# Four graph layers on one core: middle biases moved from TensorE to VectorE, a leak made of two exponentials, unsplit scores, spread weight splits and new orders

## The reference

```python
# layer 0: hypergraph convolution, H = (adj != 0)
h = relu(Dn * (H @ (Be * (H.T @ (x @ W1.T)))) + b1);  h = layer_norm(h) * gamma + beta
y = Dn * (H @ (Be * (H.T @ (h @ W2.T)))) + b2 + x
# layer 1: GCN with tanh;     tanh(dinv * A @ dinv * (x @ W) + b)
# layer 2: attention
s = (x @ w) @ a;  A = s[:, None] + s[None, :];  A = tanh(A / 8) * 8
A = where(A >= 0, A, 0.1 * A);  A = exp(A) * adj;  A = A / A.sum(-1) * adj.sum(-1);  out = A @ x @ w
# layer 3: three adjacency products with a weight each, biases after each, relu after the first two
x1 = relu(adj @ (x @ W1) + b1);  x2 = relu(adj @ (x1 @ W2) + b2);  out = adj @ (x2 @ W3) + b3
```

## Time and profile before

| | |
|---|---|
| median of 3 runs | 1438.51 us |
| the profiled execution | 1435.79 us |
| its span, first to last instruction | 1433.8 us |
| mean granted TensorE clock | 0.995 |
| busy: PE, DVE, ACT, POOL | 1392.3, 1287.9, 990.5, 947.7 us |
| instructions: PE, DVE, ACT, POOL | 10900, 4001, 2312, 1876 |

### The profile page before, as it was taken

One profiled execution on the slowest core, in us unless ns is written; L12 is line 12 of the kernel. 1 busy time (PEld: TensorE's weight loads), 2 busy tenths in 40 slices (PEclk: granted clock), 3 DMA queues, 4 the chain that ended last, 5 costly groups with the idle time before them and its releaser, 6 DMA issues.

```text
span 1433.8 us, 34585 instructions
## 1 busy us (share of the span) xinstructions
PE 1392.3 (97%) x10900; PEld 1331.7 (93%) x10900; DVE 1287.9 (90%) x4001; ACT 990.5 (69%) x2312; POOL 947.7 (66%) x1876
## 2 busy tenths in 40 slices
PE   3799999999999999999999999999999999999997
PEld 2799999999999999999999999999999999999996
DVE  5789999999999999999999999999999999999984
ACT  3577777777777777777777777777777777777763
POOL 2676676676676676676676676676676676676652
PEclk9999999999999999999999999999999999999999
DMA  7011110120110110110110110110110110110100
GB/s 187 1 42 27 52 51 26 51 51 26 51 51 26 51 51 26 51 51 26 51 51 26 51 51 26 51 51 26 51 51 26 51 51 26 51 51 26 37 19 23
DMA packets 83078, 62.70 MB, mean 44 GB/s; under 512 B 40304, under 2 KB 65520, under 8 KB 83056
## 3 DMA queue, kind: packets, MB, share of 16 engines
q1 hardware_dynamic: 83056, 62.43, 15.8%
HBM read 45.62 MB, written 16.78 MB: 44 GB/s over the span
## 4 chain that ended last, share of the span: by engine, by line
PE 95%; DVE 2%; ACT 1%; issue 0%; DMA 0%; POOL 0%; SPq 0%; DVEq 0%; POOLq 0%
PE BANK L365 29%; PE BANK L330 24%; PE BANK L372 15%; PE WIDE L365 8%; PE WIDE L341 8%; PE WIDE L372 4%; PE BANK L357 2%; PE BANK L315 2%; PE BANK L384 2%; DMA TMP_D<-in_l2wt 0%; PE WIDE L278 0%; DVE BN_B L550 0%; DVE BN_C L550 0%; ACT UHI_D L444 0%; PE WIDE L284 0%
## 5 line engine op out<-in xcount | busy, mean ns | idle before, releaser
L444 ACT ACTIVATE UHI_B<-BANK 128x512 fp32r<-128x512 f32 x96 | 57.0, 593 | 43.9 <-PE BANK L330 43.9
L444 ACT ACTIVATE UHI_D<-BANK 128x512 fp32r<-128x512 f32 x96 | 57.1, 595 | 41.1 <-PE BANK L330 41.1
L444 ACT ACTIVATE UHI_C<-BANK 128x512 fp32r<-128x512 f32 x96 | 57.0, 594 | 41.0 <-PE BANK L330 41.0
L444 ACT ACTIVATE UHI_A<-BANK 128x512 fp32r<-128x512 f32 x96 | 57.1, 594 | 39.1 <-PE BANK L330 39.1
L599 DVE TENSOR_TENSOR ULO_D<-BANK,UHI_D 128x512 fp32r<-128x512 f32 x96 | 65.2, 680 | 18.7 <-ACT UHI_D L444 18.0
L732 POOL TENSOR_TENSOR LN_A<-MV_A,EPS 128x2 f32<-128x2 f32 x80 | 15.9, 198 | 92.3 <-DVE MV_A L558 92.3
L599 DVE TENSOR_TENSOR ULO_A<-BANK,UHI_A 128x512 fp32r<-128x512 f32 x96 | 65.2, 680 | 12.3 <-ACT UHI_A L444 11.8
L599 DVE TENSOR_TENSOR ULO_C<-BANK,UHI_C 128x512 fp32r<-128x512 f32 x96 | 65.1, 678 | 11.1 <-ACT UHI_C L444 9.3
L599 DVE TENSOR_TENSOR ULO_B<-BANK,UHI_B 128x512 fp32r<-128x512 f32 x96 | 65.7, 684 | 10.4 <-ACT UHI_B L444 8.5
L732 POOL TENSOR_TENSOR LN_D<-MV_D,EPS 128x2 f32<-128x2 f32 x80 | 15.8, 197 | 84.7 <-DVE MV_D L558 84.7
L732 POOL TENSOR_TENSOR LN_B<-MV_B,EPS 128x2 f32<-128x2 f32 x80 | 16.7, 209 | 78.2 <-DVE MV_B L558 78.2
(11 more groups left out here) (500 smaller groups left out, 6009.6 us busy)
## 6 DMA issues: line engine op xcount, KB each, us to landing
X_A<-in_xs SPq DMA_DIRECT2D x16, 256.0 KB, 2.8
X_B<-in_xs SPq DMA_DIRECT2D x16, 256.0 KB, 2.8
X_C<-in_xs SPq DMA_DIRECT2D x16, 256.0 KB, 2.8
X_D<-in_xs SPq DMA_DIRECT2D x16, 256.0 KB, 2.8
out_rows<-O_A SPq DMA_DIRECT2D x16, 256.0 KB, 2.0
out_rows<-O_B SPq DMA_DIRECT2D x16, 256.0 KB, 2.1
out_rows<-O_C SPq DMA_DIRECT2D x16, 256.0 KB, 2.1
out_rows<-O_D SPq DMA_DIRECT2D x16, 256.0 KB, 2.1
```

The lines of the kernel that those rows point to most:

```text
L444: nc.scalar.activation(UHI[s][:, 0:J * D], bank(s, step)[:, :], ACT.Copy).then_inc(sem(f"c{step}"), 1)
```

## The change

- 4W and 5W lose the bias matmul. DVE adds the bias from a 128x256 row tile to the bank and writes `H` (new turns 4W and 5W on DVE), and ACT does the relu in place on `H`. The bank is free after DVE's add.
- The scores are not split: turns 2H and 2L go, and 3S is two full fp32 matmuls against `IDENT`.
- The leak: ACT takes exp(8 t) to PSUM and exp(0.8 t) in place, and DVE takes the greater of the two.
- Two small DVE instructions with a constant (TC, L570, and the first of DA, L579) become a greater-of-two-tiles with a tile of constants.
- The lump `last_weights` is gone; the splits are single pieces between turns. `low_weights("0W")` stays after A TB, but the spread vectors and `W2G` move behind A DD, `centred_weights` behind A 0W, and PE's `shifts` behind A 0W.
- All tables of slots are new.

```diff
 PE_SLOTS = {
+    "G": 5.03, "0U": 18.28, "0W": 23.04, "1U": 29.55, "1W": 34.98, "2U": 45.66, "2W": 48.39, "3S": 63.29,
+    "3U": 68.21, "3W": 70.61, "4U": 83.87, "4W": 86.20, "5U": 89.28, "5W": 91.09, "6U": 93.96, "6W": 100.54}
 DVE_SLOTS = {
+    "T": 3.90, "X": 4.63, "TC": 8.47, "TB": 12.57, "XA": 14.25, "DA": 18.63, "DB": 18.99, "DC": 20.57, "DD": 30.10,
+    "0U": 32.13, "0W": 35.26, "0S": 36.47, "0A": 37.90, "1U": 42.66, "1W": 49.42, "1S": 50.94, "1A": 52.77,
+    "2U": 59.47, "2W": 61.69, "2S": 64.38, "2A": 64.62, "2N": 71.31, "3L": 77.37, "3R": 78.92, "3E": 79.04,
+    "3U": 82.01, "3I": 83.33, "3J": 84.12, "3W": 84.15, "3S": 84.54, "3A": 84.64, "4U": 94.08, "4W": 98.78,
+    "5U": 102.44, "5W": 104.12, "6U": 107.62, "6W": 109.61}
 POOL_SLOTS = {
+    "N0": 4.66, "AT": 18.88, "RX": 19.83, "RB": 26.07, "NZ": 27.29, "RH": 29.33, "DI": 36.07, "N1": 41.34,
+    "2A": 49.38, "N2": 50.94, "2S": 60.59, "N3": 72.68, "X3": 79.13}
...
-                    if biased:
-                        nc.tensor.matmul(to[:, :], SHARES[:, :], BIAS[step][:, :, :], start=True, stop=False)
...
             def spread_scores(s, c, k):
-                pe.wait_ge(sem("scores_split"), c["n1"])
+                pe.wait_ge(sem("s_ready"), c["n1"])
                 bank_free(s, "3S", k)
                 for j in range(J):
-                    for part in (SHI, SLO):
-                        last = nc.tensor.matmul(bank(s, "3S")[:, j * P:(j + 1) * P], part[s][:, j:j + 1].to_broadcast([P, P]),
-                                                IDENTR[:, :], start=(part is SHI), stop=(part is SLO))
+                    last = nc.tensor.matmul(bank(s, "3S")[:, j * P:(j + 1) * P], ST[s][:, SC, j:j + 1].to_broadcast([P, P]),
+                                            IDENT[:, :], start=True, stop=True)
...
             def scores_exp(s, c, k):
-                act.wait_ge(sem("scores_leak"), c["n1"])
-                to = bank(s, "3S")[:, 0:J * P]
-                nc.scalar.activation(to, to, ACT.Exp, scale=8.0).then_inc(sem("e_ready"), 1)
+                act.wait_ge(sem("scores_tanh"), c["n1"])
+                nc.scalar.activation(bank(s, "3S")[:, 0:J * P], AE[s][:, :, :], ACT.Exp, scale=8.0)
+                nc.scalar.activation(AE[s][:, :, :], AE[s][:, :, :], ACT.Exp, scale=8.0 * LEAK).then_inc(sem("both_exp"), 1)
...
-                    act.wait_ge(sem(f"p{step}"), c["n1"])
-                    nc.scalar.activation(H[s][:, :, :], bank(s, step)[:, :], ACT.Relu).then_inc(sem(f"c{step}"), 1)
+                    act.wait_ge(sem(f"b{step}"), c["n1"])
+                    nc.scalar.activation(H[s][:, :, :], H[s][:, :, :], ACT.Relu).then_inc(sem(f"c{step}"), 1)
...
-                nc.vector.tensor_scalar(ST[s][:, CNM, :], ST[s][:, CNT, :], 1.0, None, ALU.max).then_inc(sem("cnm"), 1)
+                nc.vector.tensor_tensor(ST[s][:, CNM, :], ST[s][:, CNT, :], ONE[:, :], ALU.max).then_inc(sem("cnm"), 1)
...
+            def biased(step):
+                def f(s, c, k):
+                    dve.wait_ge(sem(f"p{step}"), c["n1"])
+                    rows = bank(s, step)[:, :].rearrange("p (j d) -> p j d", j=J)
+                    nc.vector.tensor_tensor(H[s][:, :, :], rows, pair(BIAS[step][:, :]), ALU.add).then_inc(sem(f"b{step}"), 1)
...
             def leak(s, c, k):
-                dve.wait_ge(sem("scores_tanh"), c["n1"])
-                nc.vector.scalar_tensor_tensor(bank(s, "3S")[:, 0:J * P], AE[s][:, :, :], LEAK, AE[s][:, :, :], ALU.mult,
-                                               ALU.max).then_inc(sem("scores_leak"), 1)
+                dve.wait_ge(sem("both_exp"), c["n1"])
+                to = bank(s, "3S")[:, 0:J * P]
+                nc.vector.tensor_tensor(to, to, AE[s][:, :, :], ALU.max).then_inc(sem("e_ready"), 1)
...
-            run(act, ACT_ORDER, parts, {("A", "0U"): lambda: high("1W", "w2c_ready", 1), ("A", "0W"): high_rest})
+            run(act, ACT_ORDER, parts, {
+                ("A", "0W"): lambda: high("1W", "w2c_ready", 1), ("A", "0Z"): lambda: high("2W", "weights_loaded", 5 * 16),
+                ("A", "1U"): lambda: high("3W", "weights_loaded", 5 * 16), ("A", "1W"): lambda: high("4W", "weights_loaded", 5 * 16),
...
-            run(dve, DVE_ORDER, parts, {("A", "TB"): first_weights, ("A", "0U"): centred_weights, ("A", "0S"): last_weights})
+            dve.wait_ge(sem("ones_ready"), 2)
+            run(dve, DVE_ORDER, parts, {
+                ("A", "TB"): lambda: low_weights("0W"), ("A", "DD"): spread_vectors, ("A", "0W"): centred_weights,
+                ("A", "0A"): lambda: low_weights("1W"), ("A", "1U"): lambda: low_weights("2W"),
+                ("A", "1A"): lambda: low_weights("3W"), ("A", "2U"): lambda: low_weights("4W"),
+                ("A", "2W"): lambda: low_weights("5W"), ("A", "2A"): lambda: low_weights("6W")})
```

More of the change, by code:

```diff
@@ L82, in program @@
         B2, L1B, L3B1, L3B2, L3B3 = (sb(n, [P, D]) for n in ("B2", "L1B", "L3B1", "L3B2", "L3B3"))
-        BIAS = {step: sb(f"BIAS{step}", [P, J, D], F32R) for step in ("4W", "5W")}
-        SHARES = sb("SHARES", [P, P], F32R)
+        BIAS = {"4W": L3B1, "5W": L3B2}
         BW = sb("BW", [P, D])
@@ L93, in program @@
         JUNK = sb("JUNK", [P, J, P])
[L94 removed]
+        MONE, MHALF, EIGHTH, EPS, ONE, LEAST = (sb(n, [P, J]) for n in ("MONE", "MHALF", "EIGHTH", "EPS", "ONE", "LEAST"))
         def per_stream(name, *shape, dt=F32):
@@ L285, in shifts @@
                 last.then_inc(sem("shift_products"), 1)
-            FREED = {"G": "cG", "3S": "sums_done", **{step: f"l{step}" for step in U_STEPS}, **{step: f"c{step}" for step in W_STEPS}}
+            FREED = {"G": "cG", "3S": "sums_done", **{step: f"l{step}" for step in U_STEPS}, **{step: f"c{step}" for step in W_STEPS},
+                     "4W": "b4W", "5W": "b5W"}
             FREED_BY = {"c0W": J, "l1U": J, "c1W": J, "c2W": J, "c3W": J}
@@ L365, in f @@
                                 nc.tensor.matmul(dst, UHI[s][:, at[m]:at[m] + P], w[:, m, :],
-                                                 start=(w is lo and m == 0 and not biased), stop=False)
+                                                 start=(w is lo and m == 0), stop=False)
                         if step == "1W":
@@ L372, in f @@
                             last = nc.tensor.matmul(dst, ULO[s][:, at[m]:at[m] + P], hi[:, m, :], start=False,
-                                                    stop=(m == chunks - 1 and (j == J - 1 or not biased)))
+                                                    stop=(m == chunks - 1))
                         if step == "0W" or j == J - 1:
@@ L396, in _ @@
                 **{step: weigh(step) for step in W_STEPS}}
-            run(pe, PE_ORDER, parts, {("A", "0U"): shifts, ("A", "0W"): lambda: pe.wait_ge(sem("shifts_ready"), 1)})
+            first = [x[:2] for x in PE_ORDER if not x[2]]
+            last_free = first[[n for n, x in enumerate(first) if x[1] in WIDE_STEPS][1] - 1]
+            run(pe, PE_ORDER, parts, {("A", "0W"): shifts, last_free: lambda: pe.wait_ge(sem("w2c_ready"), 1)})
         @block.scalar
@@ L403, in high @@
                 nc.scalar.activation(WHI[step][:, :, :], RAW[step][:, :, :], ACT.Copy).then_inc(sem("weights_high"), 1)
-            def high_rest():
-                for step in W_STEPS[2:]:
-                    high(step, "weights_loaded", 5 * 16)
             def normalise(src, dst, ready, done):
@@ L525, in centred_weights @@
                 last.then_inc(sem("w2c_ready"), 1)
-                nc.vector.tensor_scalar(SHARES[:, :], ONES[:, :], 2 / P, None, ALU.mult).then_inc(sem("shifts_ready"), 1)
-            def last_weights():
-                low_weights("1W")
-                dve.wait_ge(sem("bias_loaded"), 6 * 16)
-                for step, row in (("4W", L3B1), ("5W", L3B2)):
-                    for j in range(J):
-                        last = nc.vector.tensor_copy(BIAS[step][:, j, :], row[:, :])
-                last.then_inc(sem("bias_high"), 1)
-                dve.wait_ge(sem("bias_high"), 1)
-                for step, row in (("4W", L3B1), ("5W", L3B2)):
-                    for j in range(J):
-                        rest = BIAS[step][P // 2:P, j, :]
-                        nc.vector.tensor_tensor(rest, row[P // 2:P, :], rest.bitcast(F32), ALU.subtract)
-                for step in W_STEPS[2:]:
-                    low_weights(step)
             def stats(src, tag, ready=None):
@@ L697, in _ @@
                      "1A": aggregate("1"), "2W": gcn_out, "2S": stats(RES, "2", "x2_ready"), "2A": aggregate("2"),
[L698 removed]
+                     "2N": node_scores, "3L": leak, "3E": attend, "3R": attention_sums,
                      "3I": sums_inverse, "3J": sums_ratio, "3W": attention_out, "3S": stats(RES, "3", "c3W"),
[L700 to L702 removed]
+                     "3A": aggregate("3"), "4W": biased("4W"), "5W": biased("5W"), "6W": last_out, **{step: low(step) for step in U_STEPS}, "1U": low_hidden}
+            dve.wait_ge(sem("ones_ready"), 2)
```

(1 more changed line is left out.)

36 lines of the change are left out of this document (10 added, 26 removed), and 11 rows, old and new, of tables (ACT_SLOTS, DVE_SLOTS).

## The result

The kernel after takes 1449.58 us (median, 1448.71 to 1450.68; four runs) against 1437.88 us for the kernel before, taken beside it (four runs): ratio 1.0082, 95% interval 1.0064 to 1.0099. It is 0.8% slower, outside my range of 1391 to 1431. The profiled execution took 1450.13 us.

The account below looks back on a forecast made before the run. PE was taken to pace the steady state. From 1435.8 us, terms -27.6, -3.0, +2.3 and +0.3 sum to -28.0, giving 1407.8; with the median's 2.7 above it the forecast was 1411 us, range 1391 to 1431.

Parts of the forecast that it names:

- the first pass's setup: DVE's split pieces in the first pass, 0.69 us each, sit before turns that wait for PE: cost 0.
- Bias matmuls: Eight PE matmuls of 0.23 us leave each pass (4W and 5W, four streams): 1.84 us a pass, -27.6 in fifteen.
- Holes and all else in the loop: PE's 0.17 us waits for ULO close at 2W, those at 5W stay or grow: -3 us, bounds -18 and +15.
- Spread scores: In 3S, two full fp32 matmuls cost about what four fp32r ones did (0.48 us): 0.
- Leak: A second exponential on ACT, about 0.42 us, replaces DVE's slow leak of 1.42 between 3S and 3U: cost 0.
- TC: Small DVE instruction that took up to 1.30 us beside POOL: falls to a mean of 0.14 to 0.2.
- the first rival: POOL holds TC, so ULO for 0W is late and PE waits 0.95 us each quarter: +57, 1468 us; chance 0.10.
- The rule that I had weighed: A DVE instruction with two SBUF inputs is held while POOL reads SBUF, so the new TC is held as before.
- DVE's sum: DVE's busy time falls by 7 us a pass to about 73 of 84: it does not become the bound.
- Place of the bias add: 5U waits for DVE's add and ACT's relu, covered by PE's list: cost 0; uncovered, 0.7 us eight times a pass.
- Head: Before D's first 1U: A's 1U waits through stream B's X load, 39.9 instead of 37.2 us; net +2.3.
- Tail: Behind the loop, D's bare 4W and 5W wait for the add: +0.8, C +0.4, other bias matmuls -0.9; net +0.3 us.

Follow-up runs that it names:

- e1: Kernel after with 30 small VectorE instructions added in the first pass, ahead of the loop; 1407.11 us, ratio 0.976 to the kernel before.
- e3: Kernel before with 200 small VectorE instructions added in the first pass, nothing changed in the loop; 1473.56 us, ratio 1.0224.
- e4: Kernel after with the 4W and 5W biases again as TensorE matmuls, and 22 small VectorE instructions added in the first pass; 1435.02 us, ratio 0.9956.
- e8: Kernel of e1 with the scores split as before the change, and 20 small instructions instead of 30; 1422.66 us, ratio 0.9911.
- e7: Kernel of e1 with the leak as before the change, on VectorE between the tanh and one exponential; 1412.65 us, ratio 0.9839.
- e6: Kernel of e1 with TC and the first instruction of DA back in their scalar form with a constant; 1407.7 us, ratio 0.9806.
- e12: Kernel before with only the 4W and 5W biases moved to VectorE, at slots 91.00 and 95.00 of the old list; 1604.29 us, ratio 1.1167.
- e5: Kernel of e1 with VectorE's first pass reordered: stream B's T, X, TC and TB stand behind A 0W; 1398.61 us, ratio 0.9743.
- e2: As e1, but with 100 small VectorE instructions in the first pass of the kernel after; 1425.1 us, ratio 0.9894.

## Why the prediction was wrong

The step that failed is the one on the first pass's setup: "The split pieces that come later (0.69 each) sit in front of turns that wait for PE; cost 0." The sum had no term for what else the rebuilt setup changes, and gave no reason for leaving it out. I followed DVE's instructions by their time and never by their number. Taking 30 of them out of the first pass moved the loop to a place where it no longer fits what DVE holds of its program, and DVE stood 3.7 us (2.25 + 1.37 in the pass shown) at each return. e1 gives the size: 1449.6 less 1407.1, 42 us, and e3 shows the same cause at work in the kernel before. With that one cause gone the kernel lands 4 us under my 1411. That closeness is partly luck: in e1 the loop gained more than I had (38.7 us in fifteen passes, not 30.6), and tail and head lost more (6.6 and 4.7, not 0.3 and 2.3).

The terms, one by one, against e1 where the stall would hide them:

- *Bias matmuls*, -27.6: right. 1.94 a pass by e4 (I had 1.84), 29 us in fifteen.
- *Holes and all else in the loop*, -3: too small. e1's pass is 2.58 under before, so 0.64 is left beside the bias, 9.6 us; the bound was -18. By step, from start to the next step's start, 2W takes 0.59 less a pass, 3S 0.45, 0W 0.39 and 1U 0.31; against that 4W (beside its bias) takes 0.61 more, 6W 0.50 and 4U to 6U 0.39. Rows of 5W in e1 show the hole of the earlier trace rows closed, where I had said that those of 5W stay:

```profile
446.19 0.40 PE L359 MATMUL BANK<-WHI5W,UHI_B 128*128 128x256 f32 x2
446.42 0.40 PE L366 MATMUL BANK<-WHI5W,ULO_B 128*128 128x256 f32 x2
446.66 0.40 PE L359 MATMUL BANK<-WLO5W,UHI_B 128*128 128x256 f32 x2
```

- *Spread scores*, 0: wrong. 3S went from 0.48 to 0.37 us, 0.45 a pass or 6.7 in all, and in the new order the split would cost 0.84 a pass more (e8). I compared 3S with itself in the old trace and took the matmul's own cost, not what it costs among its neighbours.
- *Leak*, 0: wrong by 0.34 a pass (e7).
- *TC*: 0.15, as forecast, and the first rival (late ULO behind a held TC) did not come. e6 shows why: POOL no longer works beside it. The rule that I had weighed could not decide here, since neither form was held. But DVE is still held elsewhere: 2N, with two tiles as input, is over 0.7 us in 65 of 128 cases in e1, each time with a long POOL instruction already running, and in 2 of 128 before (its rows stand with the profile after).
- *DVE's sum*, 73 us a pass: too low. e1 has 1155.96/1250 x 83.4 = 77.1. What leak, TC and cast gave back, 2N took in part, 3.7 us a pass. PE did not wait for it in the loop.
- *Place of the bias add*, "cost 0": right in the new order. The price without cover, "0.7 us eight times a pass", was far too low. It counted the path and not DVE's queue ahead of the add; in the old order the wait was 2.67 us (e12).
- *Head*, +2.3: right, +2.6 for D's 1U. For A's 1U 39.9 was forecast and 40.0 measured, through B's X as written; e5 takes that path away and gains 8. The hit to 0.1 us is partly luck: `ULO` of A came at 22.2 where I had 23.5 and `centred_weights` ended at 32.5 where I had 33.5, and POOL's steps behind took the microsecond back.
- *Tail*, +0.3: wrong, +5.8. With the bias back on PE (e4) the tail is 1433.3 - 1379.0 = 54.3 against 52.3 before, so the new order costs 2.0. The rest is 2.5 in e5 (56.8) and 4.6 in e1 (58.9), where the granted clock was lower for longer. The wait before a U step grew from 0.69 to 1.44 at four places of three streams, and I had counted one stream in full.

The parts taken back singly from e1 sum to 1.94 + 0.84 + 0.34 = 3.1 us a pass, more than the 2.6 between before and e1. If the parts simply add, the new orders alone, with the old parts, would be no faster than the old ones; this is worked out, and was not run.

## What to carry to other kernels

When an edit changes how many instructions an engine has ahead of a hardware loop, look at the queue of instruction pieces in the trace after. Pieces that land once in each pass, beside waits put down to "issue" at the loop's top, cost microseconds at every return (1.2 to 3.0 here). Small instructions in an idle stretch of the first pass can take them away, if their number is right: here 30 and 158 did, 100 did not. Judge an edit only once both versions are free of this, or the alignment's 42 us will be read as the edit's. And price an operation moved to a busy in-order engine by what stands ahead of it in that queue, not by its own length.

## What the runs showed of the hardware

- DVE is held where a long POOL instruction was already running. Before, the leak took 1.4 us or more in 45 of 64 cases; in each a POOL instruction of over 1.15 us had started ahead of it. In 15 cases such a one started behind it: the leak took 0.42, and POOL's 1.28 us mostly grew to 1.5. So it matters which started first. Beside small POOL instructions alone (0.7 us and less) the leak was never held, before or in e7. With a long one ahead TC was held in 60 of 61 cases before, and 2N in 65 of 66 in e1. The cast of the scores was held (0.73) beside small ones too; why it differs from the leak is not shown.
- The stall's size varies with the place: 3.7 us a pass in the kernel after (of which 2.0 reached PE's 3S), 2.4 in e2, 3.1 in e3. The passes grew by 3.0, 1.2 and 2.4.
- In the middle of the tail PE's granted clock fell in the kernel after and in e1, and not in e5. Inside the first stretch below e1 has 0.51 from 1373.4 to 1376.8, the lower of the two levels (1.2 GHz); e5 falls to it only from 1390 on. Stretches of ten us, first e1, then e5, in the columns of the earlier trace rows:

```profile
1367.60:1377.60 10.00, 6.49 (x36) 5.60 (x36) 5.62 (x19) 5.18 (x15) 3.79 (x10) 0.83 0.07 26
```

```profile
1359.50:1369.50 10.00, 6.39 (x45) 5.59 (x46) 6.22 (x21) 5.25 (x15) 3.81 (x10) 1.00 0.07 26
```

The tails differ by 58.9 - 56.8 = 2.1 us though the lists are the same. PE did 36 matmuls in the one stretch and 45 in the other, busy for about the same time. The four runs of e1 part in the same way: 1408.3 and 1408.5 us at a mean clock of 0.992, 1405.6 and 1405.9 at 0.995 and 0.996. In both stretches PE had just waited 1.6 us for Z_D, so that wait alone does not make the clock fall; what does stays open.
